# A four-layer graph network on one core: weights before two x loads, a first product in a new order, a last unit in three parts, and new order tables

## The chip, the cores and the metric

The kernel runs on one core of a Trainium2 chip. The metric is the device time of one execution in microseconds, as the median of several executions. Lower is better.

## The reference

The input is x of shape (8, 1024, 128), a batch of eight, and one adjacency matrix adj of 1024 x 1024, mostly zeros. Four layers follow each other, each with a residual sum and a normalisation over the last axis:

```python
x = norm(x + adj @ (x @ W0) + b0)                                   # layer 0
x = norm(x + ((si + sj + adj * w_r + g_b) @ x) @ W1 + b1)           # layer 1, si and sj are row and column terms
x = norm(x + attention(x, adj))                                     # layer 2: elu, sigmoid gates masked by adj, elu
h = x                                                               # layer 3: a GRU-like cell, five steps
for step in range(5):
    m = adj @ h                                                     # the same adj for "in" and "out"
    z = sigmoid(m @ (w3a + w3b) + h @ u3 + bz)
    r = sigmoid(m @ (w4a + w4b) + h @ u3 + br)
    v = tanh(m @ (w5a + w5b) + (r * h) @ u5 + bv)
    h = (1 - z) * h + z * v
out = norm(x + h)
```

## The kernel before, in words

**Precision by parts.** A float32 factor is split into a high part that TensorE can multiply in its faster float32r form, and a low part, the difference. ScalarE makes the high part (a copy), VectorE the low part (`lo`, L1359). A product is then three float32r passes (high x high, high x adj_lo, low x adj_hi): `adj_product` (L808) for products with adj, eight tiles of adj times three passes into one PSUM bank of 512 columns, and `passes` (L817) for products with a weight. adj itself is loaded once, in eight row tiles, and split into `adj_hi` and `adj_lo`.

**Pieces.** The work of layers 0 to 2 on one batch is cut into pieces, named by two or three letters and the batch: x0 (high and low part of x), c0/c2 (bias added to x), m0a/m0b and m1a/m1b (the halves a and b of the product with adj in layers 0 and 1), y0, y1, y2 (the product with the weight and the residual sum), v0 to v2 (statistics), n0 to n2 (POOL's reciprocal root and ScalarE's normalisation), l1 and d1 (low part and row dots for layer 1), sums and rows (small products of layer 1), t2, pj, th, tg, as, ax (projection and attention terms of layer 2), s, q and e followed by half and tile (ScalarE's sigmoid and VectorE's masking of one mask tile, its split, and TensorE's product with it), rs and rv (row sums, and the layer's inner product with its elu). `events` (L265) says which engines a piece has work on.

**Units.** Layer 3 is 40 units: four pairs of batches, five steps, two batches in turn. A unit (`unit` on each engine: L1068, L1301, L1633) makes half product 0 with adj, the previous unit's candidate, half product 1, and the gates. Between its parts stand numbered slots (`fill`), into which pieces of later batches are put. For slots of TensorE's unit 0: 0 to 8 lie in and just behind product 0, 9 to 17 in and behind product 1, 19 behind the products with the state, 20 and 21 behind the update gates. Unit 1, the second batch of the first pair, has as its inputs xh and xl, which ScalarE and VectorE make at the end of their unit 0 (`start_natural`, L1218 and L1562) from the batch's normalised x (piece n2:1).

**What sets the order.** The order of each engine's work is written out by hand in `TABLES` (L30 to L262), one table for each of SyncE (SP), TensorE (PE), ScalarE (ACT), VectorE (DVE) and POOL: the line `first` holds the pieces before unit 0, and each line `unitN` the pieces for its slots. Each engine runs strictly in its order and waits on semaphores. `bank_free` and `before_set` add the waits for PSUM banks. The tables are the only place in which due times are kept; nothing is planned at run time.

**The start.** SP issues x of batch 0, the eight tiles of adj, x of batch 1, W0, x of batches 2 and 3, and then six weight loads (L715 to L727). TensorE's product m0:0 goes through adj's tiles as they come (L1101 to L1108), after `s_al`, the low part of the tile. VectorE's piece `weights` (L1393) adds weight halves, waits for ScalarE's high part `wh` and makes `wl`.

**The ending.** The last unit has its own function (`ending`: L1048, L1281, L1669): two halves of 512 columns, in which the candidate of half 0 is made while half 1 is in work. Batch 7 is put out in two parts (`OUTPUTS`, L534): statistics, POOL's root, and the normalisation by ScalarE for part 0 and by VectorE for part 1 (L1694), then the store.

Of the kernel before, what the change touches and what calls it, by code (L numbers as in the profile page):

```python
# [76 lines left out]
first m0a:0 m0b:0 m0a:1 y0a:0 y0b:0 m0b:1 y0a:1 y0b:1 m0a:2 m0b:2 m1a:0 m1b:0 sums:0 m1a:1 rows:0 y1a:0  # L77
first m1b:1 y1b:0 sums:1 y0a:2 y0b:2 rows:1 y1a:1 y1b:1 t2a:0 t2b:0 pja:0 pjb:0 tha:0 thb:0 tga:0 tgb:0
first m1a:2 e00:0 e01:0 e02:0 t2a:1 e03:0 m1b:2 e04:0 e05:0 t2b:1 e06:0 e07:0 pja:1 rsa:0 sums:2 rva:0 e10:0
first e11:0 e12:0 y2a:0 pjb:1 e13:0 e14:0 e15:0 rows:2 y1a:2 tha:1 thb:1 y1b:2 tga:1 e16:0 tgb:1 e17:0 rsb:0  # L80
first rvb:0 e00:1 e01:1 e02:1 e03:1 e04:1 e05:1 e06:1 y2b:0 e07:1 m0a:3 e10:1 e11:1 e12:1 m0b:3 e13:1 e14:1
# [9 lines left out]
unit8 @4 e07:3 @5 rva:3 @11 y2a:3 e10:3 @17 e11:3 @18 e12:3 @21 e13:3
unit9 @4 e14:3 @10 e15:3 @16 e16:3 rsb:3 e17:3 @17 rvb:3 @22 y2b:3
unit10 @21 m0a:4 @26 m0b:4
unit11 @1 y0a:4 @3 y0b:4 @22 m1a:4 @24 m1b:4 @26 sums:4
unit12 @15 rows:4 @21 y1a:4 @22 y1b:4
unit13 @19 m0a:5 @22 m0b:5 pja:4 y0a:5 pjb:4 @23 y0b:5 @26 th0:4 th1:4
unit14 @3 th2:4 @11 m1a:5 @18 m1b:5 e00:4 sums:5 e01:4 e02:4 e03:4 @21 e04:4 e05:4 rows:5 @22 e06:4
unit15 @8 e07:4 y1a:5 rsa:4 @12 e10:4 e11:4 e12:4 rva:4 @22 y1b:5 e13:4
# [2 lines left out]
unit18 @12 e00:5 @17 e01:5 @18 e02:5 @19 e03:5 @25 e04:5 @26 e05:5 e06:5
unit19 @1 e07:5 rsa:5 @8 e10:5 e11:5 e12:5 rva:5 e13:5 @9 e14:5 @10 e15:5 @11 y2a:5 @14 e16:5 @15 e17:5 rsb:5 @16 rvb:5 @22 y2b:5
unit20 @21 m0a:6 @26 m0b:6
unit21 @1 y0a:6 @3 y0b:6 @22 m1a:6 @24 m1b:6
unit22 @9 sums:6 @13 rows:6 @18 y1a:6 @21 y1b:6
unit23 @21 m0a:7 @23 m0b:7 pja:6 y0a:7 pjb:6 @24 y0b:7 @27 th0:6
unit24 @6 th1:6 @10 th2:6 @11 m1a:7 @19 m1b:7 @22 e00:6 e01:6
unit25 @1 e02:6 sums:7 e03:6 e04:6 @3 e05:6 @5 e06:6 e07:6 @11 rsa:6 rows:7 @17 e10:6 e11:6 @22 y1a:7 e12:6 rva:6 e13:6 @25 e14:6 @27 y2a:6
unit26 @4 e15:6 @6 y1b:7 e16:6 @10 rsb:6 @12 e17:6 @16 rvb:6 @22 y2b:6
unit27 @13 pja:7 @14 pjb:7 @21 th0:7 th1:7 @23 th2:7  # L110
unit28 @12 e00:7 @17 e01:7 @18 e02:7 @19 e03:7 @25 e04:7 @26 e05:7 e06:7
# [13 lines left out]
first x0:0 x0:1 x0:2 m0a:0 weights:0 m0b:0 m0a:1 m0b:1 n0:0 m0a:2 n0:1 m0b:2 m1a:0 m1b:0 m1a:1 m1b:1 n1:0
first t2a:0 t2b:0 pja:0 pjb:0 n0:2 tha:0 thb:0 tga:0 n1:1 tgb:0 s00:0 s01:0 s02:0 m1a:2 s03:0 s04:0 s05:0
first t2a:1 s06:0 m1b:2 s07:0 t2b:1 e07:0 s10:0 s11:0 s12:0 pja:1 rva:0 s13:0 s14:0 s15:0 pjb:1 s16:0 s17:0
first tha:1 thb:1 tga:1 tgb:1 e17:0 s00:1 s01:1 s02:1 rvb:0 s03:1 s04:1 s05:1 s06:1 n1:2 s07:1 x0:3 e07:1
first s10:1 s11:1 s12:1 m0a:3 n2:0 s13:1 s14:1 s15:1
# [1626 lines left out]
```

## Time and profile before

| what | value |
|---|---|
| median of 3 runs | 1237.68 us (1237.33 to 1238.51) |
| profiled execution | 1235.95 us, with a span of 1234.0 us from its first to its last instruction |
| TensorE (PE) busy | 1172.3 us, 95% |
| VectorE (DVE) busy | 927.5 us, 75% |
| ScalarE (ACT) busy | 684.7 us, 55% |
| POOL busy | 74.5 us, 6% |
| granted TensorE clock, mean | 0.988 of full speed |

The busy times are those of one execution. The 1.95 us between its time and its span lie around the program. A row of the timeline has the start and the duration in us, the engine (PEld is TensorE's weight load, SPq a DMA issue by SyncE), the line of the kernel, the operation, what it writes and reads, and in brackets how long the engine was idle before it and what ended that. Since matmuls are pipelined, the duration of one is longer than the distance from one to the next. Lines of helpers (L813, L818 to L820, L824, L831, L1128, L1359) stand for many places, which are told apart by the tiles. The `ones` tile that the change's filler products read is set on POOL at 3.05 to 3.27 us.

### The profile page before, as it was taken

The numbers are of one execution on the slowest core, as the hardware profiler recorded it, in microseconds if no ns is written. First come the engines' busy times: TensorE is split into PE (matmuls) and PEld (weight loads), VectorE is DVE, ScalarE is ACT, GpSimd is POOL, SyncE is SP. The second block draws the span as 40 slices with busy tenths as digits, with TensorE's granted clock in tenths as the row PEclk, the third lists the DMA queues.
The fourth block names the chain that finished last, engine by engine and source line by source line (L and its number), as shares of the span: only waits on it lengthen the run. The fifth ranks groups of instructions, "written<-read, shape, count | busy, mean of one in ns | idle before, by whom it ended". The sixth has DMA issues, their size and how long they took to land.

```text
span 1234.0 us, 15530 instructions
## 1 busy us (share of the span) xinstructions
PE 1172.3 (95%) x5232; PEld 907.4 (74%) x5232; DVE 927.5 (75%) x2071; ACT 684.7 (55%) x1119; POOL 74.5 (6%) x80
## 2 busy tenths in 40 slices
PE   7979899799999999999999999999999999999995
...
GB/s 249 87 76 94 102 112 1 34 120 78 94 94 85 95 86 88 41 77 60 92 96 78 128 94 69 69 52 52 104 111 86 111 78 86 18 1 1 1 1 35
DMA packets 92575, 93.66 MB, mean 76 GB/s; under 512 B 9104, under 2 KB 62992, under 8 KB 92496
## 3 DMA queue, kind: packets, MB, share of 16 engines
...
q8 instruction: 42, 0.69, 0.2%
...
## 4 chain that ended last, share of the span: by engine, by line
PE 58%; DVE 22%; ACT 6%; issue 4%; DMA 4%; SPq 4%; POOL 2%; DVEq 0%; POOLq 0%; ACTq 0%
PE ps L813 33%; PE ps L818 4%; PE ps L820 4%; PE ps L819 4%; PE ps L936 4%; DVE ring L1544 3%; PE ps L831 3%; ACT x L1133 3%; DMA mk<-mask_scratch 2%; SPq L693 2%; DVE tl L1359 2%; DVE hT L1598 1%; DVE v L1595 1%; PE ps L824 1%; DVE ml L1359 1%
## 5 line engine op out<-in xcount | busy, mean ns | idle before, releaser
L813 PE MATMUL ps<-adj_hi,xh 128*128 128x512 f32 x672 | 281.6, 419 | 13.1 <-DVE xl L1359 7.1
L813 PE MATMUL ps<-adj_hi,xl 128*128 128x512 f32 x672 | 263.0, 391 | 0.0
L813 PE MATMUL ps<-adj_lo,xh 128*128 128x512 f32 x672 | 262.5, 391 | 0.0
L813 PEld LDWEIGHTS ps<-adj_hi,xh 128*128 128x128 f32 x672 | 126.7, 189 | 50.4 <-issue 19.0
L813 PEld LDWEIGHTS ps<-adj_lo,xh 128*128 128x128 f32 x672 | 126.8, 189 | 32.6 <-issue 8.9
L813 PEld LDWEIGHTS ps<-adj_hi,xl 128*128 128x128 f32 x672 | 126.4, 188 | 27.3
L1577 DVE TENSOR_TENSOR r<-r,hT 128x512 f32<-128x512 f32 x80 | 53.7, 688 | 76.8 <-ACT r L1271 76.8
L818 PE MATMUL ps<-mh,wh 128*128 128x512 f32 x240 | 101.9, 425 | 6.7 <-DVE ml L1359 5.2
L1544 DVE TENSOR_TENSOR ring<-ring,mk 128x512 f32<-128x512 f32 x128 | 86.9, 685 | 27.2 <-ACT ring L1206 23.9
L1206 ACT ACTIVATE ring<-fh,asn 128x512 f32<-128x512 f32 x96 | 67.3, 719 | 62.6 <-DVE mk L1359 21.5
L1128 ACT ACTIVATE mh<-ps 128x512 fp32r<-128x512 f32 x80 | 47.2, 590 | 92.0 <-PE ps L813 92.0
L820 PE MATMUL ps<-ml,wh 128*128 128x512 f32 x240 | 93.8, 391 | 0.0
L819 PE MATMUL ps<-mh,wl 128*128 128x512 f32 x240 | 93.7, 390 | 0.0
L1359 DVE TENSOR_TENSOR ml<-ps,mh 128x512 fp32r<-128x512 f32 x80 | 54.9, 687 | 36.0 <-ACT mh L1128 35.8
L1271 ACT ACTIVATE r<-ps,cols 128x512 f32<-128x512 f32 x80 | 54.7, 689 | 39.6 <-PE ps L820 39.3
L1128 ACT ACTIVATE xh<-tl 128x512 fp32r<-128x512 f32 x48 | 30.2, 629 | 78.4 <-DMA tl<-state_scratch 78.2
L818 PE MATMUL ps<-th,wh 128*128 128x512 f32 x160 | 68.0, 425 | 2.7 <-DVE tl L1359 2.7
L1263 ACT ACTIVATE z<-ps,cols 128x512 f32<-128x512 f32 x80 | 53.2, 685 | 27.1 <-PE ps L820 26.8
L1552 DVE TENSOR_TENSOR fr<-fr,ring 128x512 f32<-128x512 f32 x84 | 58.2, 693 | 9.1 <-DVE ring L1544 0.5
L936 PE MATMUL ps<-ring,fz 128*128 128x512 f32 x128 | 63.8, 599 | 0.5 <-DVE ring L1544 0.2
L820 PE MATMUL ps<-tl,wh 128*128 128x512 f32 x160 | 62.7, 392 | 0.0
L819 PE MATMUL ps<-th,wl 128*128 128x512 f32 x160 | 62.6, 391 | 0.0
...
## 6 DMA issues: line engine op xcount, KB each, us to landing
mk<-mask_scratch SPq DMA_DIRECT2D x128, 256.0 KB, 2.8
...
```

Source lines behind the costliest of these rows:

```text
L813: mm = pe.matmul(dst, a[:, t, :], b[:, t, cut(h)], start=(t == 0 and i == 0), stop=(t == T - 1 and i == 2))
L818: pe.matmul(dst, wh[:, k, :], hi, start=first, stop=False, skip_group_check=True)
L819: pe.matmul(dst, wl[:, k, :], hi, start=False, stop=False, skip_group_check=True)
L820: return pe.matmul(dst, wh[:, k, :], lo, start=False, stop=last, skip_group_check=True)
L936: mm = pe.matmul(ps[:, BANKS_B[b][h], :], g, e, start=(t == 0 and i == 0), stop=False, skip_group_check=True)
L1128: return act.activation(dst, src, ACT.Copy)
L1206: tell(act.activation(ring[:, k % RING, :], f["h"][:, cut(h)], ACT.Sigmoid, bias=source[:, t:t + 1]), "sg" + name[1:], b)
L1271: act.activation(r[:, cut(h)], ps[:, GB + h, :], ACT.Sigmoid, bias=rb).then_inc(r_done, 1)
L1359: return dve.tensor_tensor(dst, src, hi.bitcast(F32), ALU.subtract)
L1544: tell(dve.tensor_tensor(ring[:, k % RING, :], ring[:, k % RING, :], mk[:, k % RING, :].bitcast(F32), ALU.mult), "ma" + name[1:], b)
L1552: tell(dve.tensor_tensor(f["r"][:, cut(h)], first_sum, ring[:, k % RING, :], ALU.add), "rs_" + name[1:], b)
L1577: dve.tensor_tensor(r[:, cut(h)], r[:, cut(h)], hT[s][:, cut(h)], ALU.mult).then_inc(rh_done, 1)
```

## The change

The order tables of all five engines are new. Beside them, in SP's issue order the six weight loads stand ahead of the loads of x of batches 2 and 3; nine products of `ones` with itself stand at TensorE's start; the first product takes each adj tile's high part first; a sixth block of weights (W4, the sum for the reset gate) is split with the others; and the last unit is cut into 512, 256 and 256 columns, each with its own banks, with ten filler products of 512 columns between its last steps. Cut to its core:

```diff
-(U3, W3, WD, W5, U5) = range(5)
+(U3, W3, WD, W5, U5, W4) = range(6)
 TABLES "PE"
-first m0a:0 m0b:0 m0a:1 y0a:0 y0b:0 m0b:1 ...
+first m0a:0 m0b:0 m0a:1 y0a:0 m0b:1 y0b:0 ...
-first m1b:1 ... t2b:0 pja:0 pjb:0 tha:0 thb:0 tga:0 tgb:0
-first m1a:2 e00:0 e01:0 e02:0 t2a:1 e03:0 m1b:2 e04:0 ...
+first m1b:1 ... t2b:0 pja:0 pjb:0 tha:0 thb:0 tga:0 m1a:2
+first tgb:0 t2a:1 m1b:2 e00:0 e01:0 e02:0 e03:0 t2b:1 e04:0 ...
-unit0 @2 rsb:1 @5 rva:1 @8 m1a:3 rvb:1 m1b:3 y2a:1 sums:3 y2b:1 rows:3 y1a:3 th0:2 @11 y1b:3 @12 th1:2 @20 th2:2
-unit1 @9 e00:2 @22 e01:2 e02:2 e03:2
+unit0 @1 e12:1 @4 e13:1 @5 e14:1 e15:1 @7 e16:1 @8 e17:1 th0:2 th1:2 m1a:3 rsa:1 m1b:3 rsb:1 sums:3 rva:1 rows:3 y1a:3 @12 y1b:3 @14 rvb:1 @19 y2a:1 th2:2 @20 y2b:1
+unit1 @9 e00:2 e01:2 @22 e02:2 e03:2 @23 e04:2
 TABLES "ACT"
-first x0:0 x0:1 x0:2 m0a:0 weights:0 m0b:0 ...
-first t2a:0 t2b:0 pja:0 pjb:0 n0:2 tha:0 thb:0 tga:0 n1:1 tgb:0 s00:0 ...
-unit0 @0 t2a:2 ... @1 n0:3 @2 rva:1 @4 m1a:3 rvb:1 m1b:3 th0:2 th1:2 n2:1 @9 n1:3 @11 th2:2
+first x0:0 x0:1 m0a:0 m0b:0 x0:2 weights:0 ...
+first t2a:0 t2b:0 pja:0 pjb:0 n0:2 tha:0 n1:1 thb:0 tga:0 m1a:2 tgb:0 t2a:1 s00:0 ...
+unit0 @0 s04:1 ... @2 s17:1 n0:3 @4 e17:1 th0:2 th1:2 m1a:3 m1b:3 rva:1 rvb:1 @6 n1:3 @9 th2:2 @14 n2:1
 TABLES "DVE"
-first x0:0 x0:1 weights:0 c0:1 c0:0 mask:0 x0:2 y0a:0 ...
-first rows:1 v0:2 c2:0 y1a:1 pja:0 pjb:0 y1b:1 v1:1 l1:2 as:0 d1:2 s00:0 ...
+first x0:0 c0:0 x0:1 weights:0 c0:1 mask:0 y0a:0 ...
+first rows:1 v0:2 y1a:1 c2:0 y1b:1 v1:1 pja:0 pjb:0 l1:2 d1:2 as:0 s00:0 ...
+unit0 @0 s04:1 ... l1:3 @2 d1:3 th0:2 rsa:1 th1:2 rsb:1 sums:3 rows:3 rva:1 y1a:3 y1b:3 v1:3 rvb:1 @4 y2a:1 y2b:1 v2:1 th2:2 @9 ax:2
 ... (units 1 to 28 of the tables likewise; the rows of units 29 to 39 stay as they were)
@@ SP
-            load(2)
-            load(3)
             ... six weight loads
+            load(2)
+            load(3)
@@ TensorE, start
+            pe.wait_ge(s_const, 1)
+            for _ in range(WARM):                  # WARM = 9
+                pe.matmul(ps[:, 7, 0:P], ones[:, :], ones[:, :], start=True, stop=True)
-            seen(pe, "xl0", 0)
+            seen(pe, "xh0", 0)
             for t in range(T):
+                pe.wait_ge(s_ah, t + 1)
+                for h in range(2):  # xh x adj_hi, then (after xl0 when t == 0) xl x adj_hi
                 pe.wait_ge(s_al, t + 1)
                 for h in range(2):
-                    for i, (a, m) in enumerate(((xh, adj_hi), (xh, adj_lo), (xl, adj_hi))):
+                    mm = pe.matmul(..., xh, adj_lo, ...)
@@ banks of the last unit: columns, then the banks of M, Z, R, V
+        LAST = ((slice(0, HALF), 2, 4, 4, 6), (slice(HALF, HALF + QUARTER), 3, 5, 0, 7),
+                (slice(HALF + QUARTER, N), 2, 1, 4, 3))
@@ TensorE, ending
+                product(0)
                 for h in range(2):
                     candidate(*prev, halves=(h,))
+                of_state(0, Z_BANK)
+                of_state(1, Z_BANK)
+                product(1, {2: lambda: update(0), 4: lambda: of_state(1, R_BANK), 6: lambda: reset(0),
+                            7: lambda: of_state(2, Z_BANK)})
+                product(2, {1: lambda: turn_state(prev[0], 0, *prev[1:]), 2: lambda: turn_state(prev[0], 1, *prev[1:]),
+                            3: lambda: reset(1), 4: lambda: update(1), 6: lambda: begin_candidate(0),
+                            7: lambda: end_candidate(0)})
+                of_state(2, R_BANK)
+                begin_candidate(1)
+                end_candidate(1)
+                reset(2)
+                update(2)
+                begin_candidate(2)
+                turn(0)
+                keep_warm(6)
+                end_candidate(2)
+                turn(1)
+                keep_warm(4)
+                turn(2)
@@ ScalarE, ending
+                split(0)
                 candidate(*prev)
+                update(0)
+                reset(0)
+                split(1)
+                round_reset(0)
+                reset(1)
+                update(1)
+                round_reset(1)
+                last_candidate(0)
+                split(2)
+                last_candidate(1)
+                reset(2)
+                update(2)
+                round_reset(2)
+                last_candidate(2)
@@ VectorE, ending
+                split(0)
                 update(*prev)
+                last_reset(0)
                 state_lo(prev[0], 0, *prev[1:])
+                last_reset_lo(0)
+                split(1)
                 state_lo(prev[0], 1, *prev[1:])
+                last_keep(0)
+                last_reset(1)
+                last_reset_lo(1)
+                last_keep(1)
                 output_stats(B - 2)
+                split(2)
+                last_update(0)
+                last_reset(2)
+                last_update(1)
+                last_reset_lo(2)
+                last_keep(2)
                 output_moments(B - 2)
+                last_update(2)
+                last_sum(0)
                 output_stats(B - 1)
                 output_moments(B - 1)
+                last_sum(1)
+                ... statistics of two tiles
+                last_sum(2)
+                ... statistics of two tiles
                 output_moments(B)
                 output_apply(B)
```

In the ending, `split` makes mh and ml of a part, `of_state`, `update`, `reset`, `begin_candidate` and `end_candidate` are three passes each over the part's columns, `turn` transposes the part of the new state, and `keep_warm(n)` issues n float32r products of 512 columns whose result nobody reads. The other new functions (`last_reset`, `last_keep`, `last_update`, `last_sum` and the like) do what `reset`, `keep`, `update` and `state_lo` did, on a part's columns.

## Rows read from the trace of the kernel before

**Rows 1.** The page: busy time and share, and 40 slices of the span.

```profile
PE 1172.3 (95%) x5232; PEld 907.4 (74%) x5232; DVE 927.5 (75%) x2071; ACT 684.7 (55%) x1119; POOL 74.5 (6%) x80
...
PE   7979899799999999999999999999999999999995
```

**Rows 2.** Windows: length, then busy us of each engine; the last three are PEclk, DMA share, GB/s.

```profile
0.00:231.00 231.00, 198.42 (x893) 144.40 (x894) 179.66 (x543) 118.61 (x199) 25.17 (x35) 0.97 0.29 96
...
231.00:1197.00 966.00, 950.50 (x4241) 745.49 (x4242) 723.25 (x1460) 550.63 (x892) 45.22 (x40) 1.00 0.23 73
...
1197.00:1234.00 37.00, 23.39 (x101) 17.52 (x99) 24.64 (x68) 15.46 (x29) 4.12 (x5) 0.82 0.10 29
...
96.00:216.00 120.00, 113.99 (x483) 76.21 (x482) 94.92 (x276) 67.35 (x110) 9.01 (x8) 0.98 0.25 79
```

**Rows 3.** Timeline of the start, with start us, duration us, engine, line.

```profile
6.24 1.06 ACT L1128 ACTIVATE adj_hi<-fh 128x1024 fp32r<-128x1024 f32 x1 [0.24 <-DMA fh<-in_adjT]
...
8.70 0.77 PE L1105 MATMUL ps<-adj_hi,fxh 128*128 128x512 f32 x1 [8.70 <-DVE adj_lo L1359]
...
12.62 0.43 PE L1105 MATMUL ps<-adj_hi,fxl 128*128 128x512 f32 x1
...
19.10 1.06 ACT L1128 ACTIVATE xh<-x 128x1024 fp32r<-128x1024 f32 x1 [0.73 <-DMA x<-in_x]
...
21.75 0.39 PE L813 MATMUL ps<-adj_hi,xh 128*128 128x512 f32 x1
```

**Rows 4.** Timeline of the weights' landing, 21 to 31 us.

```profile
21.10 0.43 SPq L727 DMA_DIRECT2D mkflat<-in_u  x1
...
21.12 1.06 ACT L1128 ACTIVATE th<-x 128x1024 fp32r<-128x1024 f32 x1 [0.97 <-DMA x<-in_x]
...
25.41 0.69 DVE L1397 TENSOR_TENSOR mkflat<-mkflat 128x128 f32<-128x128 f32 x3 [4.00 <-DMA mkflat<-in_u]
...
28.71 2.35 DVE L1444 TENSOR_TENSOR x<-x,rows 128x1024 f32<-128x1024 f32 x2
```

**Rows 5.** Timeline of TensorE at 80 to 97 us.

```profile
82.01 1.13 PE L831 MATMUL ps<-wf,z 128*128 128x128 f32 x8 [1.95 <-DVE kb L1485]
...
88.57 0.63 PE L824 MATMUL ps<-ident,fk 128*128 128x128 f32 x4 [2.20 <-DVE fk L1525]
...
93.42 3.75 PE L912 MATMUL ps<-fk,we2b 128*128 128x512 f32 x4 [3.09 <-ACT fz L1128]
...
96.18 1.42 PE L813 MATMUL ps<-adj_hi,th 128*128 128x512 f32 x1
```

**Rows 6.** Windows at 92 to 96 us, columns as in rows 2.

```profile
92.00:96.00 4.00, 2.58 (x3) 1.18 (x4) 3.80 (x26) 2.26 (x5) 1.89 (x2) 0.50 0.00 0
```

**Rows 7.** Timeline of the handover from unit 0 to unit 1.

```profile
221.74 3.18 ACT L1133 ACTIVATE x<-x,nbAp,rsAp 128x128 f32<-128x128 f32 x8
...
230.82 0.80 PE L813 MATMUL ps<-adj_hi,xh 128*128 128x512 f32 x1 [7.07 <-DVE xl L1359]
```

**Rows 8.** TensorE's waits at 231 to 1197 us: total, times, longest.

```profile
PE ps L813 <- DVE ml L1359: 5.7, 7, 2.3
```

**Rows 9.** Timeline of TensorE at the longest wait of the middle.

```profile
1054.49 0.47 PE L813 MATMUL ps<-adj_hi,xh 128*128 128x512 f32 x1 [2.28 <-DVE ml L1359]
```

**Rows 10.** Timeline of the last 15 us.

```profile
1221.42 0.79 PE L818 MATMUL ps<-th,wh 128*128 128x512 f32 x1 [2.46 <-DVE tl L1359]
...
1225.46 1.09 PE L824 MATMUL ps<-ident,hT 128*128 128x128 f32 x4 [2.39 <-DVE hT L1598]
...
1230.13 1.12 DVE L1700 TENSOR_SCALAR x<-x,mvo,rso 128x128 f32<-128x128 f32 x4 [1.12 <-POOL rso L778]
```

**Rows 11.** Chain of waits at the ending: start us, length us, what.

```profile
1197.07 5.44 PE ps L813 x24
...
1207.72 0.44 PE ps L824 x4
```

**Rows 12.** Timeline: a low part of 256 columns on VectorE.

```profile
226.81 0.41 DVE L1359 TENSOR_TENSOR fxl<-ps,gh 128x256 fp32r<-128x256 f32 x1
```

More of the change, by code:

```diff
@@ L76 @@
     "PE": """
[L77 to L81, printed above, removed]
@@ L91 @@
[L91 to L98, printed above, removed]
@@ L99 @@
-unit16 @2 e14:4 y2a:4 e15:4 e16:4 @10 e17:4 rsb:4 @15 rvb:4 @22 y2b:4
-unit17 @13 pja:5 pjb:5 @21 th0:5 th1:5 @23 th2:5
[L101 to L111, printed above, removed]
+first m0a:0 m0b:0 m0a:1 y0a:0 m0b:1 y0b:0 y0a:1 y0b:1 m0a:2 m0b:2 m1a:0 m1b:0 sums:0 m1a:1 rows:0 y1a:0
@@ new lines @@
+first m1b:1 y1b:0 sums:1 y0a:2 y0b:2 rows:1 y1a:1 y1b:1 t2a:0 t2b:0 pja:0 pjb:0 tha:0 thb:0 tga:0 m1a:2
+first tgb:0 t2a:1 m1b:2 e00:0 e01:0 e02:0 e03:0 t2b:1 e04:0 sums:2 e05:0 e06:0 e07:0 pja:1 rsa:0 rows:2
+first y1a:2 rva:0 e10:0 e11:0 e12:0 pjb:1 y2a:0 y1b:2 e13:0 e14:0 e15:0 e16:0 e17:0 rsb:0 tha:1 rvb:0 thb:1
+first tga:1 y2b:0 tgb:1 m0a:3 e00:1 e01:1 e02:1 m0b:3 e03:1 e04:1 e05:1 e06:1 y0a:3 e07:1 y0b:3 pja:2 pjb:2
+first e10:1 e11:1
+unit0 @1 e12:1 @4 e13:1 @5 e14:1 e15:1 @7 e16:1 @8 e17:1 th0:2 th1:2 m1a:3 rsa:1 m1b:3 rsb:1 sums:3 rva:1 rows:3 y1a:3 @12 y1b:3 @14 rvb:1 @19 y2a:1 th2:2 @20 y2b:1
@@ new lines @@
+unit11 @9 m0b:4 @12 y0a:4 @16 y0b:4
+unit12 @6 m1a:4 @12 m1b:4 @14 sums:4 @16 rows:4 @21 y1a:4 @24 y1b:4
+unit13 @19 m0a:5 @22 m0b:5 pja:4 y0a:5 pjb:4 @23 y0b:5 @26 th0:4
+unit14 @9 th1:4 th2:4 @11 m1a:5 @19 m1b:5 @22 sums:5 e00:4 e01:4
+unit15 @13 rows:5 e02:4 e03:4 e04:4 @14 e05:4 @18 rsa:4 @19 e06:4 @22 e07:4 y1a:5 rva:4 e10:4 e11:4 e12:4 y1b:5 @23 y2a:4 @25 e13:4
+unit16 @6 e14:4 e15:4 @9 e16:4 @10 e17:4 @14 rsb:4 @16 rvb:4 @22 y2b:4
+unit17 @13 pja:5 pjb:5 @21 th0:5 th1:5 @23 th2:5
+unit18 @18 e00:5 e01:5 e02:5 @24 e03:5 @25 e04:5 @26 e05:5 e06:5
@@ new lines @@
+unit19 @1 e07:5 rsa:5 @16 rva:5 e10:5 e11:5 e12:5 @18 y2a:5 e13:5 e14:5 @20 e15:5 @21 e16:5
+unit20 @5 e17:5 rsb:5 @8 rvb:5 @18 y2b:5 @22 m0a:6 @25 m0b:6 @27 y0a:6
+unit21 @2 y0b:6 @22 m1a:6 @24 m1b:6
+unit22 @2 sums:6 @10 rows:6 @21 y1a:6 @22 y1b:6
+unit23 @19 m0a:7 @22 m0b:7 pja:6 pjb:6 y0a:7 @24 y0b:7 @26 th0:6 th1:6
+unit24 @4 th2:6 @11 m1a:7 @18 m1b:7 @21 sums:7 @22 e00:6 e01:6 e02:6 @23 rows:7 @24 e03:6 e04:6 @25 e05:6
+unit25 @1 y1a:7 @10 y1b:7 e06:6 @18 e07:6 rsa:6 @21 e10:6 rva:6 e11:6 @24 e12:6 @26 y2a:6 e13:6 e14:6 e15:6
@@ L124 @@
     "ACT": """
[L125 to L129, printed above, removed]
@@ L191 @@
-unit13 @4 x0:5 t2b:4 c0:5 @7 c2:4 y0a:5 pja:4 pjb:4 y0b:5 v0:5 @11 th0:4 th1:4 @15 th2:4 ax:4 l1:5
-unit14 @4 d1:5 @5 s00:4 s01:4 s02:4 s03:4 sums:5 s04:4 s05:4 @7 s06:4 s07:4 s10:4 s11:4 rows:5
-unit15 @1 s12:4 rsa:4 @4 y1a:5 s13:4 s14:4 rva:4 s15:4 @7 y1b:5 v1:5 s16:4 @15 s17:4 y2a:4
+first x0:0 c0:0 x0:1 weights:0 c0:1 mask:0 y0a:0 mask:1 x0:2 mask:2 c0:2 y0b:0 y0a:1 v0:0 y0b:1 mask:3 v0:1
+first mask:4 l1:0 d1:0 l1:1 d1:1 mask:5 mask:6 sums:0 mask:7 rows:0 y1a:0 y1b:0 v1:0 sums:1 y0a:2 y0b:2
```

359 lines of the change are left out of this document (228 added, 131 removed).

## Prediction, made before the result was known

> **What bounds the kernel now.** I read the page's busy times and slices first. They show the reader a TensorE that is busy for 95% of the span in every slice but a few [rows 1]. Then I read the busy times by stretch: of 61.7 us without TensorE work, 32.6 lie before 231 us (the unit 0 to unit 1 handover ends there), 15.5 in the 966 us after it, and 13.6 in the last 37 us [rows 2]. So the kernel is bound by TensorE's work, and only three things can move its time: idle before 231 us, small waits in the middle, and the end. The change adds and removes no product outside the ending, so I count idle time and the length of the end chain. Third, the timeline around each long wait, for what came last.
>
> **The change part by part.** The sum is made on the profiled execution, 1235.95 us with a span of 1234.0; its median of runs is 1237.68, so 1.73 us are added at the end.
>
> *First product from the high part, with nine filler products ahead.* Now the first product waits for adj_lo until 8.70, although adj_hi of that tile is done at 7.30 (6.24 + 1.06), and runs at the lower clock up to 12.62 [rows 3]. In the change it can start at 7.3 and has the filler before it from about 3.3, when ones is set. But the product behind it, of batch 1, needs xl of x1. x1's xh is made at 19.10 to 20.16, because its load lands then, and VectorE puts c0:0 (one 1.2 us addition, half of the pair at 28.71 [rows 4]) ahead of xl now: adj_lo ends at 19.63, c0:0 at 20.85, xl at 22.1. TensorE starts that product at 21.75 today [rows 3]. The saved time ends in a wait: I take +0.35 us. If c0:0 ran after xl it would be 0; at best, if x1 landed a full microsecond earlier, -0.7; at worst +1.
>
> *Weights ahead of two x loads.* Their last issue is at 21.10 and VectorE waits 4.00 us, until 25.41, for them; then ScalarE's wh (27.20) and VectorE's wl, and only then the two c0 additions [rows 4]. The change issues six weight loads some 3.5 us earlier, behind x1's, so they land before VectorE comes free at 22.1. What is late next is the x2 load: ScalarE now has x0:2 ahead of the weights, x2 lands some 3 us later than its 21.12, near 24, so wh is made at 25.1 to 26.0 and wl (six blocks in place of five, +0.14 us) ends at 26.9, not 28.8. With c0:0 already done VectorE is 3 us ahead. The cover of TensorE is nearly complete there: its products of x0 to x2 run on from 21.75. What VectorE's lead can still remove of waits before 80 us is 0.3 to 1.5 us; I take -0.8. Ends: 0, if x2's later landing costs batch 2's first product the same, and -1.5.
>
> *The prologue's orders.* At 80 to 96 us TensorE waits in turn for VectorE's kb, for the projection of batch 0 and for ScalarE's copy, 1.95 + 2.20 + 3.09 us, and the last wait leaves it at the lower of its two clocks, 1.2 GHz, 0.50 granted at 92 to 96 [rows 5, 6]. The new orders put v1:1 (statistics, 2.4 us) before pja:0, but l1:2 right behind pjb:0, and m1a:2 before tgb:0. By the durations of now: pjb:0 ends at 92.5, not 89.6; l1:2 at 94.05; m1a:2 starts at 94.4 with 0.9 us of tgb:0 still to do, against 96.18 after all of it. That is -1.0 us (ends -2.5 and +2, since tha's copy is now followed on ScalarE by n1:1's 3.2 us before thb's, and the first sigmoid comes 2 us later than its 100.96). At 96 to 216 us TensorE is busy 113.99 of 120 us [rows 2], so 6.0 us is all that can be gained. VectorE is busy 94.92 there, and with two operations of 0.65 a mask tile against TensorE's 0.92 it is the slower of the two only while tiles are made; I find waits of 2 to 8 us by the new order. I take 0, ends -4 and +3.
>
> *The handover to unit 1.* Today TensorE waits 7.07 us for xl, until 230.82: behind z come n1:3 (3.18), r, th and xh on ScalarE, then xl [rows 7]. The new order moves n1:3 ahead of z and n2:1 (3.2 us) behind both th, just ahead of xh; and it moves y2a:1, y2b:1 (1.8 us each) and v2:1 behind the second product. Let P be the end of that product (215.7 now, so the start of unit 1 is P + 15.1). New: state passes 1.36, y2a 1.8, th2 0.4, gate 0.68, y2b 1.8 bring P + 6.05; sum and statistics 3.3, POOL 1.64 + 0.4, n2:1 3.2, xh 1.04, xl 1.23 bring P + 17.1, and the chain over n1:3, z with its table load, r and th reaches P + 12 before n2:1, so P + 17.5. TensorE does 9.4 us of work in it, so it idles 8.1 us against 8.66 now; P itself comes 3.6 us earlier by what is moved behind it. I take -0.5, ends -2.9 and +4.
>
> *Middle.* 15.5 us idle [rows 2], in waits of under 1 us but one; 5.7 us are product starts that wait for ml, 2.28 of them in one place behind batch 7's attention [rows 8, 9], where the rows of units 29 to 31 are unchanged. The rest depends on which piece stands where. Nothing in the rows favours the new order over the old, but some 12 us are open to it; I take -1.0, ends -5 and +5.
>
> *The last unit in three parts (512, 256, 256 columns).* Now the half product takes 5.44 us for 24 matmuls, 0.227 each, beginning at 1197.07 (call it 0); TensorE waits 2.46 us at 1221.42 for tl and 2.39 at 1225.46 for hT, the last hT ends at 1225.31 (+28.2), VectorE's last apply at 1231.25 (+34.2) [rows 10, 11]. No row has a 256-column float32r matmul. Bounds: a 128-column transpose with its own weight load has a pitch of 0.11 (the nearest row, four in 0.44 [rows 11]), a 512-column one 0.227; half of the latter plus the 13 ns that it has over 512 clocks is 0.12. I take 0.12; 0.17 would add 4 us over 84 narrow matmuls, of which some 2 lie on the chain. A 256-column low part takes 0.41 on VectorE where 512 columns take 0.69 [rows 12]; ScalarE's copies go the same way, 0.37 and 0.60. Followed through: products end at 5.4, 12.85 and, after a 1 us wait of reset(1) for ml(1) (VectorE has two earlier results to finish first, state_lo and last_reset_lo), at 19.7. Part 2 is split on ScalarE behind tanh of part 0 at 20.6, ml 21.05, r 22.15, r x h 22.85, tl 24.1 (behind both halves of last_update(1)), last passes 24.35 to 24.7, tanh 25.4, the last hT at 26.35. The chain is 1.9 us shorter. But VectorE then still holds last_sum(0) and its statistics and moments, then two sums with statistics, then the moments: 4.85 us where 3.7 stood; POOL 1.1 and apply 1.12 end it at 33.5. So -0.7 us at the store, whose cost is unchanged. The fillers (10 x 0.227 = 2.3 us) lie inside waits for hT and tl, the first six end 0.25 us late. Ends: -2.5 and +2.
>
> The Trainium skill ("TensorE: Matmul & The Clock Gate", Back-to-back issue gap) gives 262 cycles for 256 columns once warm, an estimate of 0.109 us, and by it the ending would come out some 0.5 us shorter; no row here shows it. The same page ("The HAM clock gate (the "warmup" mystery)") holds that activity releases the throttle, for which the fillers are put in; the trace agrees in that the clock is 0.50 right behind the 3.09 us wait [rows 5, 6]. By it the last passes and transposes, now 0.43 apart, would be spaced at 0.227.
>
> **Sum.** +0.35 - 0.8 - 1.0 + 0 - 0.5 - 1.0 - 0.7 = -3.65 us: 1232.3 profiled, 1234.0 as a median.
>
> **Rivals.**
> A, forecast (0.46): small gains as above, 1231 to 1236.
> B (0.20): the orders do all that their idle time leaves: a third of the 32.6 us before 231 and of the 15.5 behind, with VectorE's 3 us lead carried through. For it: long waits at 82 to 93 and at 230.82 are matters of order. Against: at 80 to 100 VectorE itself is full. 0.2 x 32.6 + 0.15 x 15.5 = 8.8 us, so 1229.
> C, slower (0.16): the handover. n2:1 stands last on ScalarE before xh. If mask tiles hold VectorE, P stays at 215.7 in spite of the moved y2 work, and unit 1 starts at 233.2; with the sigmoids of batch 0 starting 2 us later as well it is +4, so 1241.5. It decides once P comes later than 213.3 (230.8 - 17.5). For it: VectorE is at 95 of 120 us and has rows:3, y1b:3 and v1:3 in front. Against: TensorE, not VectorE, is full there.
> D (0.18): idle is only moved about; the edits at both ends do nothing, since x1's landing holds the one and VectorE's tail the other: 1236.5 to 1238.5.
>
> **How the numbers follow.** This kernel's measurement tells 0.2%, 2.5 us, from no change: faster is below 1235.2, slower above 1240.2. A lies about three quarters below 1235.2 (0.35) and the rest within (0.11); with B 0.20, faster is 0.55; same is 0.11 + 0.18 = 0.29; slower is 0.16. Predicted is A's 1234.0. A's own range is 1231 to 1236; to hold 8 in 10 it reaches most of B and into C, 1226.5 to 1240.5.
>
> **What would show it.** First product begun at 7.3 and a wait for xl near 22; mkflat's additions near 22 and not 25.41; m1a:2 (batch 2) near 94 to 95; unit 1's start between 227 and 231; 256-column matmuls 0.12 apart; the last hT 26 to 27 us after the last unit's start and some 7 us of VectorE, POOL and apply behind it. It would be wrong if unit 1 started before 226 or after 233, if middle waits changed by over 5 us, or if narrow matmuls stood 0.2 apart.

## The result and the profile after

The changed kernel takes 1243.78 us (median of 8 runs, 1239.93 to 1246.17), the kernel before in the same session 1238.03 (8 runs, 1236.18 to 1238.59): ratio 1.0041, 95% interval [1.0030, 1.0053]. That is slower by some 5 us, where 1234.0 was forecast and 1240.5 was the upper end. Its profiled execution took 1245.94 us with a span of 1244.1, near the top of its spread, so the two profiled executions differ by 10 us, where the ratio is worth 5.1 us and the medians differ by 5.75.

The page of the changed kernel answers to [rows 1]:

```profile
PE 1180.6 (95%) x5305; PEld 918.4 (74%) x5305; DVE 928.4 (75%) x2078; ACT 690.1 (55%) x1128; POOL 73.8 (6%) x80
...
PE   8979799799989999999999999999999999999996
```

Windows of the changed kernel, cut at unit 1's and at the last unit's start; columns as in [rows 2]:

```profile
0.00:234.13 234.13, 203.29 (x911) 148.44 (x911) 180.22 (x543) 125.00 (x205) 25.34 (x35) 0.97 0.29 97
234.13:1208.21 974.08, 952.07 (x4241) 748.11 (x4242) 722.75 (x1460) 548.88 (x891) 44.38 (x40) 0.99 0.22 72
1208.21:1243.00 34.79, 25.26 (x155) 21.88 (x154) 25.38 (x75) 16.24 (x34) 4.05 (x5) 0.93 0.10 30
96.00:216.00 120.00, 110.62 (x445) 72.32 (x444) 91.92 (x265) 69.44 (x107) 7.19 (x6) 0.97 0.25 79
```

Unit 1 starts at 234.13 against 230.82 [rows 7], 3.3 us later. From there to the last unit's start pass 974.08 us against 966.25 (1197.07 [rows 11] less 230.82): 7.8 more. Between 96 and 216 us TensorE idles 9.4 us where 6.0 stood [rows 2]. Not all of the 3.3 us reaches the middle: by the update gate of unit 5 (z, at 350.70 against 349.69) 1.0 us is left of it. The start and the ending do what they were meant to. Timeline of the start (each of the nine float32 filler products shows as two records), then of the weights, then of the wait ahead of the attention of batch 0:

```profile
3.32 4.21 PE L1188 MATMUL ps<-ones 128*128 128x128 f32 x18 [3.32 <-POOL ones L761]
7.36 1.19 PE L1196 MATMUL ps<-adj_hi,fxh 128*128 128x512 f32 x2
...
21.83 0.50 PE L823 MATMUL ps<-adj_hi,xh 128*128 128x512 f32 x1 [1.17 <-DVE xl L1490]
```

```profile
21.83 0.69 DVE L1528 TENSOR_TENSOR mkflat<-mkflat 128x128 f32<-128x128 f32 x3
...
25.41 0.96 DVE L1490 TENSOR_TENSOR wl<-mkflat,wh 128x768 fp32r<-128x768 f32 x1 [1.83 <-ACT wh L1228]
```

```profile
91.36 2.21 PE L834 MATMUL ps<-ident,fk 128*128 128x128 f32 x8 [5.31 <-DVE fk L1656]
...
94.29 0.84 PE L823 MATMUL ps<-adj_hi,th 128*128 128x512 f32 x1
```

The handover from unit 0 to unit 1. The first pass over the state's result stands at 216.44, some 0.2 us ahead of ScalarE's mh:

```profile
216.64 0.60 ACT L1228 ACTIVATE mh<-ps 128x512 fp32r<-128x512 f32 x1 [1.40 <-PE ps L823]
218.21 3.19 ACT L1233 ACTIVATE x<-x,nbAp,rsAp 128x128 f32<-128x128 f32 x8 [0.97 <-POOL nbAp L781]
...
228.54 3.18 ACT L1233 ACTIVATE x<-x,nbBa,rsBa 128x128 f32<-128x128 f32 x8 [0.22 <-POOL nbBa L781]
231.76 1.06 ACT L1228 ACTIVATE xh<-x 128x1024 fp32r<-128x1024 f32 x1
...
232.84 1.23 DVE L1490 TENSOR_TENSOR xl<-x,xh 128x1024 fp32r<-128x1024 f32 x1 [2.59 <-ACT xh L1228]
...
234.13 0.80 PE L823 MATMUL ps<-adj_hi,xh 128*128 128x512 f32 x1 [7.98 <-DVE xl L1490]
```

The middle has one long wait that the kernel before lacks, in unit 6, at the first aggregation product of batch 3, which stands at 364.84 without a wait in the kernel before (first block) and at 371.89 in the changed one. The chain is the store of the attention targets (issued at 358.98; before, at 351.90), their load (issued at 362.67, behind the store of a state half; before, at 354.08) and landing, ScalarE's sigmoid, VectorE's ring and mk, then TensorE. Behind the wait twelve products stand 0.43 us apart:

```profile
364.84 0.39 PE L936 MATMUL ps<-fxh,gh 128*128 128x512 f32 x1
```

```profile
358.98 1.29 SPq L664 DMA_DIRECT2D target_scratch<-att  x4
...
368.22 1.95 ACT L1306 ACTIVATE ring<-fh,asn 128x512 f32<-128x512 f32 x3 [7.61 <-DMA fh<-target_scratch]
...
369.04 1.30 DVE L1675 TENSOR_TENSOR ring<-ring,mk 128x512 f32<-128x512 f32 x2 [4.73 <-ACT ring L1306]
...
371.89 0.76 PE L946 MATMUL ps<-fxh,gh 128*128 128x512 f32 x1 [4.53 <-DVE mk L1490]
372.45 0.63 PE L946 MATMUL ps<-mk,gh 128*128 128x512 f32 x1
372.88 0.63 PE L946 MATMUL ps<-fxh,fxl 128*128 128x512 f32 x1
```

The window behind the wait, TensorE alone: length, its busy time, granted clock (0.50, that is 1.2 GHz), DMA share, GB/s:

```profile
372.00:377.00 5.00, 5.00 (x12) 0.50 0.20 66
```

The chain at the ending (start, length, what) answers to [rows 11]; narrow products (256 columns) stand 0.12 apart (six in 0.72), and the last application ends 33.1 us after the last unit's start, not 34.2:

```profile
1208.21 5.44 PE ps L823 x24
...
1224.87 0.72 PE ps L823 x6
...
1233.78 0.42 DVE hT L1833
...
1240.78 0.51 DVE x L1880 x2
```

### The profile page after: what moved, and what is told of

The parts are those of the page before. It is cut to its first block, busy times and chain, and to the rows that moved or that the text cites. A ratio compares the mean times of both kernels' runs of the same rounds, so it can differ in the third digit from the quotient of the medians.

```text
span 1244.1 us, 15699 instructions
## 1 busy us (share of the span) xinstructions
PE 1180.6 (95%) x5305; PEld 918.4 (74%) x5305; DVE 928.4 (75%) x2078; ACT 690.1 (55%) x1128; POOL 73.8 (6%) x80
## 4 chain that ended last, share of the span: by engine, by line
PE 67%; DVE 16%; ACT 6%; DMA 5%; issue 3%; SPq 2%; POOL 1%; DVEq 0%; POOLq 0%; ACTq 0%
PE ps L823 38%; PE ps L828 5%; PE ps L830 5%; PE ps L829 5%; PE ps L946 4%; PE ps L841 3%; ACT x L1233 2%; DVE ring L1675 2%; SPq L701 2%; PE ps L834 1%; DVE x L1582 1%; DVE tl L1490 1%; DVE hT L1729 1%; DMA tl<-state_scratch 1%; DMA mk<-mask_scratch 1%
## 5 line engine op out<-in xcount | busy, mean ns | idle before, releaser
L823 PE MATMUL ps<-adj_hi,xh 128*128 128x512 f32 (+1 forms) x680 | 280.9, 413 | 14.4 <-DVE xl L1490 9.2
L823 PE MATMUL ps<-adj_hi,xl 128*128 128x512 f32 (+1 forms) x680 | 264.5, 389 | 0.0
L823 PE MATMUL ps<-adj_lo,xh 128*128 128x512 f32 (+1 forms) x680 | 263.9, 388 | 0.0
L823 PEld LDWEIGHTS ps<-adj_hi,xl 128*128 128x128 f32 x680 | 127.9, 188 | 26.9
L828 PE MATMUL ps<-mh,wh 128*128 128x512 f32 (+1 forms) x243 | 105.7, 435 | 8.2 <-DVE ml L1490 6.7
L1228 ACT ACTIVATE mh<-ps 128x512 fp32r<-128x512 f32 (+1 forms) x81 | 47.4, 585 | 102.8 <-PE ps L823 102.6
L830 PE MATMUL ps<-ml,wh 128*128 128x512 f32 (+1 forms) x243 | 94.9, 390 | 0.0
L829 PE MATMUL ps<-mh,wl 128*128 128x512 f32 (+1 forms) x243 | 94.8, 390 | 0.0
L1490 DVE TENSOR_TENSOR ml<-ps,mh 128x512 fp32r<-128x512 f32 (+1 forms) x81 | 55.1, 680 | 50.8 <-ACT mh L1228 50.6
L828 PE MATMUL ps<-th,wh 128*128 128x512 f32 (+1 forms) x164 | 68.8, 420 | 0.0
L828 PEld LDWEIGHTS ps<-mh,wh 128*128 128x128 f32 x243 | 46.1, 190 | 26.4 <-DVE ml L1490 12.1
L830 PE MATMUL ps<-tl,wh 128*128 128x512 f32 (+1 forms) x164 | 63.4, 386 | 0.0
```

What stands on the lines that cost most here:

```text
L823: mm = pe.matmul(dst, a[:, t, :], b[:, t, cols], start=(t == 0 and i == 0), stop=(t == T - 1 and i == 2))
L828: pe.matmul(dst, wh[:, k, :], hi, start=first, stop=False, skip_group_check=True)
L829: pe.matmul(dst, wl[:, k, :], hi, start=False, stop=False, skip_group_check=True)
L830: return pe.matmul(dst, wh[:, k, :], lo, start=False, stop=last, skip_group_check=True)
L1228: return act.activation(dst, src, ACT.Copy)
L1490: return dve.tensor_tensor(dst, src, hi.bitcast(F32), ALU.subtract)
```

## Experiments

"Old orders" are the orders of the kernel before, "new code" is every edit outside them. The diffs are cut to their core. The kernel before stood at 1237.26 in the first session (e1 to e4), 1236.93 in the second (e5 to e8) and 1236.66 in the third; the ratios are what compares across sessions, and one thousandth is 1.24 us.

**e1_tables_before: new code, old orders.**

```diff
-TABLES = { the new orders }
+TABLES = { the orders of the kernel before }
```

> The changed kernel with the five order tables of the kernel before; start, weight loads, W4 and the ending in three parts as changed. Theory 1 (the loss is in the new orders): faster than before by what the ending gives, 1237.0, from 1236.0 to 1238.0, and some 7 us below the changed kernel. Theory 2 (the edits of the code cost, the nine products at the start, the later x loads or the narrow matmuls): 1241 or more.

1237.34 us, ratio 0.9997 [0.9987, 1.0007]. The new orders carry the whole loss; start, weights and ending together are worth nothing that can be measured. (The new orders on the old code were not run.)

**e4_ending_only: the kernel before with the ending in three parts.**

```diff
+    LAST = ((slice(0, HALF), 2, 4, 4, 6), (slice(HALF, HALF + QUARTER), 3, 5, 0, 7), ...
-                state_product(s, 0, p, i, prev, {})
+                product(0)
```

> The kernel before with the ending in three parts, its fillers and W4, and nothing else. Theory 1: last unit's start unchanged at 1197.1, the last apply ends 33.1 us behind it and not 34.2, so 1 us faster: ratio 0.9991, 1236.9. Rival (the ending's gain is eaten by W4's wider split and by the store): no change, 1238.0.

1236.96 us, ratio 0.9999 [0.9991, 1.0008]. Its trace has the last application 33.1 us after the last unit's start as well: the 1.1 us is in the trace and under the resolution of the runs, so they decide for neither expectation.

**e2_prologue_before: old orders ahead of unit 5, new from unit 5 on, new code.**

```diff
-first, unit0 ... unit4: new
+first, unit0 ... unit4: as in the kernel before
```

> The changed kernel with the rows of before for everything ahead of unit 5; from unit 5 on the new rows. Theory 1 (3.3 us of the loss arise before unit 1, about 5 in units 5 to 7 by the late landing of batch 3's targets, 3 in units 12 to 24): unit 1 starts near 230.8 to 231, the time is 1240.5 (1239 to 1242.5), and the wait for the first sigmoid of batch 3 near 365 us is there in some executions. Rival (all is the prologue's): 1237.

1241.93 us, ratio 1.0040 [1.0027, 1.0054]: nearly all of the loss without one new row ahead of unit 5. Its trace has the same wait in unit 6, 3.70 us for mk at 368.77.

**e3_targets_early: the changed kernel with unit 5 as before and tga:3, tgb:3 back in it.**

```diff
-unit5 @5 ax:3
-unit6 @2 tga:3 tgb:3 @5 k03:3 ...
+unit5 @5 ax:3 tga:3 tgb:3
+unit6 @5 k03:3 ...
```

The lines are SP's; the rows of unit 5 on TensorE, ScalarE and VectorE are the old ones as well.

> The changed kernel, but with unit 5's rows of before, so that th2 and ax of batch 3 stand one slot earlier and SP issues tga and tgb of batch 3 in unit 5, not behind the sending of a state half in unit 6. Theory 1: ScalarE's 7.6 us wait for the targets at 368 and TensorE's 4.5 us wait at 372 go; the median falls by 3 to 5 us to 1239.5, and the spread of 6 us between executions falls to 2. Rival (the landing is late by contention with the state's eight loads, whichever slot): no change, 1243.5 with the same spread.

1240.27 us, ratio 1.0028 [1.0017, 1.0040], 1.3 thousandths or 1.6 us under the changed kernel where 3 to 5 us were expected; the intervals overlap, so the gain isn't clear of the noise, and its six runs range over 4.2 us, not 2. In the trace ScalarE's wait of 7.61 us is gone, the sigmoids start at 358.92, and yet TensorE waits at the same place, now for ml:

```profile
358.92 1.94 ACT L1306 ACTIVATE ring<-fh,asn 128x512 f32<-128x512 f32 x3
363.33 0.63 ACT L1228 ACTIVATE fxh<-ring 128x512 fp32r<-128x512 f32 x1 [2.48 <-DVE ring L1675]
366.62 0.63 ACT L1228 ACTIVATE xh<-tl 128x512 fp32r<-128x512 f32 x1 [2.65 <-DMA tl<-state_scratch]
367.15 0.58 ACT L1228 ACTIVATE mh<-ps 128x512 fp32r<-128x512 f32 x1
```

```profile
368.63 0.80 PE L828 MATMUL ps<-mh,wh 128*128 128x512 f32 x1 [2.16 <-DVE ml L1490]
```

ScalarE's xh stands ahead of its mh and waits for the returned state, and mh waits behind it. That order is not new (the kernel before has xh at 368.46, mh at 368.99, and a wait for ml of 0.95 us). What is new is TensorE's cover: the kernel before has three aggregation products of batch 3 ahead of the pass that waits for ml (at 364.84, 367.85 and 368.65), the new unit 6 has one (365.62), and the other two stand behind it. So TensorE comes to that pass earlier and waits longer. By this trace the moved target loads are one cause in that block and the moved aggregation products another; no run moves the latter alone.

**e5_new_until_4: new orders ahead of unit 5, old from unit 5 on, new code.**

```diff
-unit5 ... unit39: new
+unit5 ... unit39: as in the kernel before
```

> The changed kernel with the rows of the kernel before from unit 5 on; the new rows stay for everything ahead of unit 0 and for units 0 to 4. Theory 1, costs add: the kernel with only the new rows from unit 5 on stood 4.6 us over the one with none of them (1241.93 and 1237.34) and the changed kernel some 6 us over it, so the new early rows carry 1.5 to 3 us by their own, through the state pass that starts at 216.4 in place of 212: 1239 to 1240.5, with unit 1 starting near 234 and the stretch between units 6.1 and 7.0 as before. Theory 2, all of the loss is in the rows from unit 5 on: 1237.0 to 1238. Theory 3, my forecast's sign for the early rows (handover -0.5, orders at 80 to 96 -1.0): 1236 or less.

1237.93 us, ratio 1.0003 [0.9991, 1.0014]: theory 2. It also shows the handover again: the state product is done at 213.5, unit 1 starts at 231.22, 17.7 us behind it as in the changed kernel.

**e6_new_until_9: new orders up to unit 9, old from unit 10 on.**

```diff
-unit10 ... unit39: new
+unit10 ... unit39: as in the kernel before
```

> The changed kernel with the rows of the kernel before from unit 10 on. Theory 1: the loss of the later rows sits in units 5 to 9, where batch 3's targets land late (+4 us between units 6.1 and 7.0), and the rows from unit 10 on cost under 1.5 us: this kernel within 1.5 us of the changed one, 1242.5 to 1244. Theory 2: the losses of the middle are spread over all phases (waits of 0.5 to 1.6 us at some ten places after 480): this kernel 3 us or more below the changed one, 1240 to 1241.

1241.23 us, ratio 1.0036 [1.0021, 1.0051]. The time lies between the two expected ranges; by the ratio it is 0.6 us under the changed kernel, within theory 1's 1.5. Against e5, on the same chip, units 5 to 9 cost 3.3 us by the medians, and the wait is back (3.78 us for mk at 370.60). It has e5's orders up to unit 4, yet reaches unit 1 2.8 us later. Some 1.3 us of this is there ahead of the wait at 147 (it ends at 148.73, in e5 at 147.40); for the rest the windows show where, e5 first, then e6, then the changed kernel, and last the kernel before; columns: window, its length, TensorE busy, granted clock, DMA share, GB/s:

```profile
150.00:160.00 10.00, 10.00 (x40) 1.00 0.40 134
```

```profile
150.00:160.00 10.00, 9.06 (x29) 0.83 0.32 111
```

```profile
150.00:160.00 10.00, 10.00 (x29) 0.71 0.40 134
```

```profile
150.00:160.00 10.00, 9.72 (x39) 0.87 0.32 107
```

The waits between 130 and 150 us are the same in the first three (2.05 us at 147.4 to 148.7 the longest), but the clock that is granted behind them is not. A granted 0.71 over 10 us is 2.9 us of work not done, which is the whole difference in the start of unit 1 between e5 and the changed kernel. It is not the difference to the kernel before, which was granted 0.87 in this window with its own orders: e5's execution is the one that was spared.

**e9_undo_5_to_9: the changed kernel with units 5 to 9 as before.**

```diff
-unit5 ... unit9: new
+unit5 ... unit9: as in the kernel before
```

> The changed kernel with one block of its orders undone: rows of units 5 to 9 as in the kernel before, everything else new. Theory 1, most of the loss sits there: 3 to 4 us under the changed kernel, 1239 to 1240 (ratio to the kernel before 1.001 to 1.002), with no wait of 3.5 us or more near 370 and the clock there at 1.00. Theory 2, the rows from unit 10 on are as bad: 1241.5 or more.

1238.82 us, ratio 1.0016 [1.0004, 1.0029], 2.5 thousandths or 3.1 us under the changed kernel, whose interval begins at 1.0030: theory 1. No wait over 1.2 us near 370, clock 1.00:

```profile
367.97 0.50 PE L946 MATMUL ps<-fxh,gh 128*128 128x512 f32 x1 [0.81 <-DVE mk L1490]
...
370.77 0.50 PE L828 MATMUL ps<-mh,wh 128*128 128x512 f32 x1 [1.14 <-DVE ml L1490]
```

```profile
362.00:380.00 18.00, 16.01 (x69) 1.00 0.33 103
```

**e10_mid_filler: the changed kernel with 18 products of no use in the 4.53 us wait.**

```diff
                         bank_free(name[:2], b)
+                        if (b, h) == (3, 0):
+                            for _ in range(18):
+                                pe.matmul(ps[:, BANKS_B[b][h], :], wh[:, U3, :], gh[:, 0:4, :]..., start=True, stop=True)
```

> The changed kernel with 18 products of no use (256 to 512 columns each in 0.23 us, 4.1 us) put ahead of the first aggregation product of batch 3, where its profile shows TensorE idle for 4.53 us and then 5 us at the granted clock 0.50. They write a bank that the next product starts anew. Theory 1, half of the middle's loss is the clock that falls after the wait: the clock stays at 1.00 behind it and the kernel is 2 to 2.5 us faster than the changed one, 1241 to 1241.8. Theory 2, the clock has another cause or the products delay what follows: no gain, 1243 to 1245.

1240.83 us, ratio 1.0032 [1.0020, 1.0044], 0.9 thousandths or 1.1 us under the changed kernel's 1.0041; the intervals overlap, so no gain is shown, but theory 1's gain of 2 us isn't excluded either. The clock did what theory 1 says, and in the trace the time followed in part:

```profile
366.58 4.24 PE L939 MATMUL ps<-gh,wh 128*128 128x512 f32 x18
370.66 0.39 PE L950 MATMUL ps<-fxh,gh 128*128 128x512 f32 x1
...
372.19 0.50 PE L828 MATMUL ps<-mh,wh 128*128 128x512 f32 x1 [0.69 <-DVE ml L1494]
...
374.79 0.51 PE L950 MATMUL ps<-fxh,gh 128*128 128x512 f32 x1 [0.94 <-DVE mk L1494]
```

At full clock TensorE runs into VectorE again, 0.69 + 0.94 us here. From the last pass ahead of the wait to the third aggregation product it takes 10.6 us (366.35 to 376.98), and 11.8 in the changed kernel (366.98 to 378.80): 1.2 us gained, where the low clock had cost some 2.8 (5.7 us at 0.50, from 371.89 to 377.57).

**e7_n1_late: the kernel before, one piece moved.**

```diff
-unit0 ... n2:1 @9 n1:3 @11 th2:2
-unit1 @1 s00:2 ...
+unit0 ... n2:1 @11 th2:2
+unit1 @0 n1:3 @1 s00:2 ...
```

> The kernel before with one edit: ScalarE's 3.2 us piece n1:3 goes from unit 0 to the start of unit 1, behind the split of the state that opens it. Theory 1, the handover is a chain on ScalarE from the first state pass at 215.7 to unit 1 at 230.8, with this piece (221.74, 3.18 us) in it: unit 1 starts near 227.7 and the kernel is 2 to 3 us faster, 1234.3 to 1235.5. Theory 2, the piece is hidden or what it feeds (its transfers of adjacency rows for batch 3) is needed early: 1237, no change, or a new wait in unit 1.

1234.76 us, ratio 0.9982 [0.9971, 0.9994], in theory 1's range. The 3.17 us piece now runs behind xh, and TensorE's wait is 5.45 us, not 7.07 [rows 7]. That is 1.6 us less and not 3.2, and unit 1 starts at 229.38 where 227.7 was expected, since ScalarE's r, no longer behind the piece, waits 1.26 us for TensorE's reset gate:

```profile
225.96 1.04 ACT L1128 ACTIVATE xh<-x 128x1024 fp32r<-128x1024 f32 x1
226.91 3.17 ACT L1133 ACTIVATE x<-x,nbAp,rsAp 128x128 f32<-128x128 f32 x8
```

```profile
229.38 0.80 PE L813 MATMUL ps<-adj_hi,xh 128*128 128x512 f32 x1 [5.45 <-DVE xl L1359]
```

**e8_n1_late_new_code: the same on the new code.** The edit is that of e7.

> The same edit of the orders on the changed kernel's code (weights ahead of two loads, first product from the high part, last unit in three parts with filler products), with the orders of the kernel before otherwise. By theory 1 the handover gains as in the kernel beside it and the ending's 1.1 us comes on top where it shows: 1233.5 to 1235. By theory 2 1237. If the new code is worth nothing in the time, the two are equal within 0.5 us.

1234.86 us, ratio 0.9980 [0.9968, 0.9992]: equal to e7, so the new code is worth nothing here either.

**e11_handover_filler: e8 with 22 products of no use ahead of unit 1.**

```diff
+                if i == 0 and p == 0 and s == 1 and h == 0:
+                    pe.wait_ge(ml_done, nth(*prev[1:], prev[0], 1))
+                    for _ in range(22):
+                        pe.matmul(ps[:, MB, :], wh[:, U3, :], mh[:, cut(0)], start=True, stop=True)
```

> Orders of the kernel before with n1:3 at the start of unit 1, the changed kernel's code, and 22 products of no use in TensorE's 5.45 us wait ahead of unit 1 (5.0 us at 0.23). Without them this kernel stood at 1234.86 with the clock at 0.50 from 228 to 233, where 11 products of 512 columns and 4 of 128 took 5.2 us and would take some 2.9 at 1.00. Theory 1, the wait costs its length and then 2.3 us of clock: 1232.3 to 1233, the best so far. Theory 2, the products only displace the fall of the clock or delay the start: 1234.5 to 1236.

1234.09 us, ratio 0.9976 [0.9963, 0.9990], the lowest of all, but not told apart from e8, and between the two expected ranges. The products fill the wait and the clock stays at 1.00:

```profile
222.32 5.15 PE L995 MATMUL ps<-mh,wh 128*128 128x512 f32 x22
227.93 0.50 PE L825 MATMUL ps<-adj_hi,xh 128*128 128x512 f32 x1 [0.47 <-DVE xl L1496]
228.27 0.39 PE L825 MATMUL ps<-adj_lo,xh 128*128 128x512 f32 x1
...
237.23 0.47 PE L948 MATMUL ps<-fxh,gh 128*128 128x512 f32 x1 [1.93 <-DVE mk L1496]
```

```profile
220.00:246.00 26.00, 23.24 (x104) 1.00 0.16 51
```

The first products are 0.23 apart where e8's were 0.43, and 9 us on TensorE waits 1.93 us for mk and then 0.37 for ml, at places where e8 did not wait: 2.3 us, what the clock had cost. The next wait of unit 1 then ends at the same time in both kernels, e8 first:

```profile
249.07 0.50 PE L948 MATMUL ps<-fxh,gh 128*128 128x512 f32 x1 [0.83 <-DVE mk L1492]
```

```profile
249.14 0.50 PE L948 MATMUL ps<-fxh,gh 128*128 128x512 f32 x1 [0.83 <-DVE mk L1496]
```

So the clock's 2.3 us had been hidden behind VectorE, and theory 1 took it for a gain.

**e12_ending_no_filler: e4 without its ten filler products.**

```diff
-                keep_warm(6)
-                keep_warm(4)
```

> The kernel before with the ending in three parts, without the ten filler products of it (with them 1236.96, which was 0.3 us under the kernel before, and last unit's start to the last application 33.1 us in place of 34.2). Theory 1, the fillers hold the clock through the two waits of the ending: without them the last turns and weights run at 0.50 and the time is 0.5 to 1.5 us longer. Theory 2, the waits are too short for the clock to fall before the end: within 0.5 us.

1236.66 us, ratio 0.9993 [0.9980, 1.0007] against e4's 0.9999: theory 2, the fillers of the ending are worth nothing that can be measured. One of the twelve executions, the profiled one, took 4191 us; the other eleven lie from 1234.03 to 1239.16, with a median of 1236.29. So what the clock did in the ending without fillers isn't known.

## Why the prediction was wrong

*The account.* In thousandths of the time before, times 1.24 us: orders ahead of unit 5, e5 less e1, 0.6 or 0.7 us, within both intervals; units 5 to 9, e6 less e5 3.3 and changed less e9 2.5, so 3.1 to 4.1 us (by medians on one chip 3.3); units from 10 on, e9 less e5 1.3 and changed less e6 0.5, so 0.6 to 1.6 us, within overlapping intervals; the code outside the orders, e1, nothing. The parts are differences along the way from e1 to the changed kernel, so that they add up is no test. What is clear of the noise is the block of units 5 to 9, on both ways.

*Steps that held.* Start: the filler began at 3.32 (3.3 forecast), the first product at 7.36, and the wait for xl ended at 21.83 (22.1). Weights: their additions at 21.83, wl done at 26.4 (26.9). Orders at 80 to 96: m1a:2 at 94.29 (94.4). Handover chain: from the state product P to unit 1 17.7 us (17.5), with n2:1 just ahead of xh as described, idle 7.98 of 17.7 us (8.1). Ending: narrow products 0.12 apart, last hT at +26.0 (26.35), the end 1.1 us shorter (0.7). The Trainium skill ("TensorE: Matmul & The Clock Gate", Back-to-back issue gap) has 262 cycles for 256 columns, an estimate of 0.109 us for the narrow products; the trace has 0.12, and the measurement decides. None of these gains shows in the runs: e1 and e4 are within a thousandth of the kernel before, with intervals of about a thousandth to each side.

*Step that failed first: the middle, "Nothing in the rows favours the new order over the old ... I take -1.0".* This term had the wrong sign and carried most of the loss. I gave 966 us one number with ends of 5 and no reason for its sign, when the diff names what is late in unit 6: the target loads tga:3 and tgb:3 move from unit 5 to unit 6, th2:3 and ax:3 to a later slot, and two aggregation products of batch 3 move behind the pass that waits for ml. In the trace the store of the targets is issued 7.1 us later (1.0 of it because unit 5 is that much later), TensorE waits 4.53 us and then has twelve products at 0.43 instead of 0.23. Undoing the block gives 3.1 us back (e9); putting unit 5 and the loads back gives 1.6, not clear of the noise (e3), and leaves a wait of 2.16 us for ml. That the block carries the loss is shown; how it is split between the late targets, the moved aggregation products and other rows of units 5 to 9 is read from the traces and was not tried.

*Step that failed second: "P itself comes 3.6 us earlier", with 0 for the orders at 96 to 216.* P came at 216.44 in the profile, 0.7 later than 215.7, so 4.3 us were missed. Most of it is waits: idle at 96 to 216 went from 6.0 to 9.4 us, 3.4 more. The two longest waits of the changed kernel that the kernel before lacks stand ahead of tgb:1 and of m0a:3:

```profile
147.59 1.10 PE L922 MATMUL ps<-v,we2b 128*128 128x512 f32 x2 [2.05 <-ACT hT L1228]
149.80 0.77 PE L823 MATMUL ps<-adj_hi,th 128*128 128x512 f32 x1 [1.11 <-DVE tl L1490]
```

The clock adds little: by windows of 1 us, the time at 0.50 between 96 and 216 cost 3.4 us of work in the changed kernel and 2.7 in the kernel before. That e5, with the same orders and the clock at 1.00, has P at 213.5 tells how far one execution lies from another, not what the change did. Even e5's P is 0.2 us past the point where rival C decides (213.3), and its unit 1 starts 0.4 us later than before: C's mechanism happened, and it was small. C's figure, 1241.5, was the nearest of the four, but for the wrong reason: e5 shows that the early orders cost at most some 1.7 us (the upper end of its interval), and C had nothing on unit 6. (Rival B's words take a third of the idle time, its sum 0.2 and 0.15 of it; by a third it would have been 16 us, so near 1222. It was far off either way.)

*Spread.* The changed kernel's eight runs range over 6.2 us, the eight of the kernel before in that session over 2.4. But in the three sessions of the experiments, with 22, 35 and 35 runs, the kernel before itself ranges over 4.0, 8.5 and 7.8 us, so that the change widens the spread isn't shown. One source of spread is seen: with the same orders up to unit 4, the stretch from 150 to 160 was granted 1.00, 0.83, 0.73 and 0.71 in four profiles (e5, e6, e9, changed). How much of the spread it explains is open.

*The clock.* Fillers held it in both places, as the rule that activity releases the throttle has it (the Trainium skill, "TensorE: Matmul & The Clock Gate", The HAM clock gate (the "warmup" mystery)); the trace agrees, 1.00 behind e11's and e10's waits against 0.50 at 372 to 377 without. Neither saved time beyond the measurement's reach. In the traces e11's fillers gained nothing and e10's 1.2 us, since VectorE is as late as before.

*What the rows did hold.* The handover's chain was read off the trace before: n1:3, 3.18 us on ScalarE, between z and r [rows 7]. Moving only that (e7) gives 2.2 us, more than the whole change was forecast to bring in the handover. The kernel before has two such pieces in the chain, n2:1 ahead of mh (215.60, 3.20 us) and n1:3 behind z; the new orders kept both there and only changed their places, to ahead of z and ahead of xh. Idle in the handover came out at 7.98 against 8.66, as forecast.

Open: the split within units 5 to 9, the 0.6 to 1.6 us of the units from 10 on, and why a wait of the same length is followed by different clocks.
